# An expert-routed low-rank FFN: summing the extension's partial groups on GpSimd and choosing the expert on 32 partitions

## The chip, the cores and the metric

The kernel runs on one core of a Trainium2 chip. The metric is its device time in microseconds (us). The profile is of one execution of the program.

## The reference

x has 8 batches of 512 tokens with 2048 features. Each batch has an adapter (a LoRA pair chosen by an index). What is computed:

```
y   = x W^T + b + 2 (x A_slot) B_slot          # conditioning layer, rank 16
lg  = y route_w^T                              # 8 experts
e   = argmax(lg) ; w = lg[e]                   # top 1, first of equals
out = x + w * ((y A_e^T) Bw_e^T)               # rank 16 per expert
```

All of it is fp32 to a precision that needs products split in a high and a low part.

## The kernel before, in words

**Algebra.** y is never formed. P is the stack of the 8 experts' A (128 rows, "ER") and of route_w (8 rows), 136 columns in all ("PN"). A first stage computes M = W^T P^T (2048 x 136) from W in 32 pieces (lines 497 to 510), with `pt` as the moving operand. The 128 expert columns are split into `m_hi` and `m_lo` (fp32r), the 8 routing columns go to columns 0 to 7 of `ext` (two buffers), and the batch's LoRA A (16 columns) goes to columns 8 to 23 of it (GpSimd, line 292). A small matrix G per batch (`g_a`, `g_route`) carries the logits' unit rows, the LoRA B times P and the bias's products; its rows repeat with each 32-row group. It is made between pieces 23 and 24 of W (lines 527 to 537 on TensorE, 402 to 408 on VectorE), from `bp` and from `gz`.

**Units.** The second stage runs over 9 units: 7 batches of 512 tokens and the last batch in two halves of 256. x lies transposed: features on partitions, tokens along the free dimension. A batch has 8 pairs of 128-feature chunks. For a unit TensorE does, in this order (lines 561 to 622):

- the extension: 16 fp32 matmuls of 32 stationary columns, spread over four column groups so that `bank_e` holds four partial sums, one for each 32 rows (line 573);
- for each pair j = 0 to 7: six fp32r matmuls to `bank_h` (588 to 590: high by high, high by low, low by high), and from j = 1 on, behind them, the six matmuls of one output pair of the unit before (`out_pair`, 541 to 558), so that output pairs 0 to 5 lie beside main pairs 1 to 6;
- after j = 0: the logits, four small fp32 matmuls from `e_sb` (598). After j = 1: their transpose to tokens on partitions (604);
- after j = 7: the correction, three fp32r matmuls of G by e (608 to 610), then four transposes of `route` to `bank_r` (615), then output pairs 6 and 7 of the unit before.

**The order on the other engines** is written out by hand; each engine runs its instructions in that order and waits on semaphores.

ScalarE (354 to 377): `e_sb` from `bank_e` with the bias row's one added; x_hi of pairs 4 to 7; `logt_sb`; `e_hi` at j = 5; x_hi of the next unit's pairs 0 to 3; `h_sb` from `bank_h`; `wh_hi`. x_hi has a ring of four slots, and a slot is free when the main pair that read it is done (`t_main`).

VectorE (470 to 491): for j = 0 to 7 one x_lo (pairs 4 to 7 of this unit, then 0 to 3 of the next, line 425), from j = 1 to 6 one add (`add_x`, 465: output pair j - 1 plus x, which frees its bank), and at j = 1 `choose` (435 to 449: maximum over 8 logits, equality, preference for the first, one hot, times the maximum), at j = 3 `e_lo`. Then `weigh` (455), add 6, `wh_lo`, add 7. Pairs on `bank_out` use two banks in turn: an output pair may start when the pair two before it has been added (`pairs_added`, 197 to 203).

The sync engine's queue (228 to 255) loads W, then x in pieces of two pairs into a ring of 12, and stores the ring's pieces when both pairs are added.

## Time and profile before

| | |
|---|---|
| device time, median of 3 runs | 304.76 us (304.1 to 304.79) |
| span of the profiled execution | 302.6 us |
| TensorE matmul, busy | 295.9 us (98%) |
| VectorE, busy | 193.1 us (64%) |
| ScalarE, busy | 99.0 us (33%) |
| GpSimd, busy | 11.0 us (4%) |
| HBM | 54.60 MB read, 33.55 MB written, 291 GB/s |

The span runs from the first to the last instruction; the time outside it, some 2 us, is launch and end. The busy time of matmuls has their latency in it, and consecutive ones overlap in the record (each lasts 0.39 us and the next starts 0.23 us later), so a pace is read from starts. The trace gives each instruction with its start, its duration, its line and its tile, and in brackets the engine's idle time before it with what ended it. Line 382 and line 309 are helpers (VectorE's subtraction, ScalarE's copy): there the tile tells what it is.

### The profile page before, as it was taken

How to read it: one execution, taken by the hardware profiler on the slowest of the kernel's cores; microseconds unless marked ns; L12 is line 12 of the kernel's file. 1: busy time of each engine (PE TensorE's matmuls, PEld its weight loads, DVE VectorE, ACT ScalarE, POOL GpSimd, SP SyncE). 2: the span in 40 equal slices, each digit the busy share in tenths (PEclk: the TensorE clock that was granted, in tenths of full speed). 3: DMA queues.
4: the chain of work that ended last, by engine and by line, in shares of the span. 5: the costliest groups of instructions: out<-in, count | busy, mean ns of one | idle time of the engine just before them, and what ended most of it. 6: DMA issues, size and time to landing. Idle time of an engine off the chain costs nothing.

```text
span 302.6 us, 4629 instructions
## 1 busy us (share of the span) xinstructions
PE 295.9 (98%) x1857; PEld 233.5 (77%) x1857; DVE 193.1 (64%) x258; ACT 99.0 (33%) x147; POOL 11.0 (4%) x37
## 2 busy tenths in 40 slices
PE   7899999999999999999999999999999999999994
PEld 4899999997675885788488758866884787787994
DVE  0160000242894997498579839984985796698775
ACT  0020000223874332534253433424342533322410
POOL 6000300000100000000000000000000000000000
PEclk9999999999999999999999999999999999999999
DMA  7999999999920067739946991998399569536468
GB/s 245 400 404 394 415 412 411 414 417 418 421 107 2 25 252 259 298 133 388 418 172 237 417 405 54 379 395 337 118 377 417 202 220 406 208 151 266 178 218 299
DMA packets 20790, 88.44 MB, mean 292 GB/s; under 512 B 2210, under 2 KB 8354, under 8 KB 12962
## 3 DMA queue, kind: packets, MB, share of 16 engines
q1 hardware_dynamic: 18464, 86.06, 72.4%
q10 hardware_dynamic: 2306, 2.10, 2.0%
q8 instruction: 14, 0.23, 0.3%
q14 instruction: 6, 0.05, 0.0%
HBM read 54.60 MB, written 33.55 MB: 291 GB/s over the span
## 4 chain that ended last, share of the span: by engine, by line
PE 92%; DMA 3%; DVE 3%; SPq 1%; issue 0%
PE bank_out L508 18%; PE bank_h L588 11%; PE bank_h L590 10%; PE bank_h L589 10%; PE bank_e L573 9%; PE bank_out L555 9%; PE bank_out L557 9%; PE bank_out L556 9%; DMA w_ring<-W 3%; DVE x_ring L465 2%; PE bank_l L521 1%; PE bank_r L615 1%; PE bank_l L598 1%; PE bank_h L608 1%; PE bank_h L610 1%; PE bank_h L609 1%
## 5 line engine op out<-in xcount | busy, mean ns | idle before, releaser
L382 DVE TENSOR_TENSOR x_lo<-x_ring,x_hi 128x1024 fp32r<-128x1024 f32 (+1 forms) x72 | 78.9, 1106 | 41.1 <-ACT x_hi L309 41.1
L309 ACT ACTIVATE x_hi<-x_ring 128x1024 fp32r<-128x1024 f32 (+1 forms) x72 | 69.2, 966 | 85.8 <-PE bank_h L590 85.8
L465 DVE TENSOR_TENSOR x_ring<-bank_out,x_ring 128x1024 f32<-128x1024 f32 (+1 forms) x72 | 79.2, 1102 | 1.4 <-PE bank_out L557 1.1
L508 PE MATMUL bank_out<-pt,w_ring 128*128 128x136 f32 x512 | 60.6, 280 | 1.4 <-DMA w_ring<-W 1.4
L508 PEld LDWEIGHTS bank_out<-pt,w_ring 128*128 128x128 f32 x512 | 59.7, 190 | 2.8 <-DMA w_ring<-W 2.5
L588 PE MATMUL bank_h<-x_hi,m_hi 128*128 128x512 f32 (+1 forms) x144 | 55.1, 383 | 0.0
L555 PE MATMUL bank_out<-wh_hi,bw_hi 128*128 128x512 f32 (+1 forms) x144 | 54.6, 379 | 0.0
L590 PE MATMUL bank_h<-x_hi,m_lo 128*128 128x512 f32 (+1 forms) x144 | 53.3, 370 | 0.0
L556 PE MATMUL bank_out<-wh_lo,bw_hi 128*128 128x512 f32 (+1 forms) x144 | 53.2, 369 | 0.0
L557 PE MATMUL bank_out<-wh_hi,bw_lo 128*128 128x512 f32 (+1 forms) x144 | 53.2, 369 | 0.0
L589 PE MATMUL bank_h<-x_lo,m_hi 128*128 128x512 f32 (+1 forms) x144 | 53.1, 369 | 0.0
L588 PEld LDWEIGHTS bank_h<-x_hi,m_hi 128*128 128x128 f32 x144 | 27.0, 188 | 13.2 <-issue 8.5
L590 PEld LDWEIGHTS bank_h<-x_hi,m_lo 128*128 128x128 f32 x144 | 27.1, 188 | 5.0
L557 PEld LDWEIGHTS bank_out<-wh_hi,bw_lo 128*128 128x128 f32 x144 | 27.1, 188 | 5.0
L555 PEld LDWEIGHTS bank_out<-wh_hi,bw_hi 128*128 128x128 f32 x144 | 27.1, 188 | 4.8
L589 PEld LDWEIGHTS bank_h<-x_lo,m_hi 128*128 128x128 f32 x144 | 27.1, 188 | 4.6
L382 DVE TENSOR_TENSOR m_lo<-bank_out,m_hi 128x256 fp32r<-128x256 f32 x8 | 3.4, 424 | 42.5 <-ACT ext L309 42.5
L556 PEld LDWEIGHTS bank_out<-wh_lo,bw_hi 128*128 128x128 f32 x144 | 27.1, 188 | 4.2
L573 PE MATMUL bank_e<-x_ring,ext 128*32 128x512 f32 (+1 forms) x288 | 29.4, 548 | 0.0
L573 PEld LDWEIGHTS bank_e<-x_ring,ext 128*32 128x32 f32 x288 | 8.4, 109 | 16.4 <-issue 15.3
L309 ACT ACTIVATE m_hi<-bank_out 128x256 fp32r<-128x256 f32 x8 | 3.1, 383 | 44.4 <-PE bank_out L508 44.4
L356 ACT ACTIVATE e_sb<-bank_e,e_bias 128x512 f32<-128x512 f32 (+1 forms) x9 | 5.8, 642 | 25.9 <-PE bank_e L573 25.9
(77 smaller groups left out, 130.1 us busy)
## 6 DMA issues: line engine op xcount, KB each, us to landing
x_ring<-xT SPq DMA_DIRECT2D x32, 1024.0 KB, 9.0
outT<-x_ring SPq DMA_DIRECT2D x28, 1024.0 KB, 5.3
w_ring<-W SPq DMA_DIRECT2D x32, 512.0 KB, 9.0
outT<-x_ring SPq DMA_DIRECT2D x16, 256.0 KB, 2.4
pt<-PT SPq DMA_DIRECT2D x4, 272.0 KB, 5.8
x_ring<-loraB ACTq DMA_DIRECT2D x8, 128.0 KB, 10.6
la<-loraA ACTq DMA_DIRECT2D x8, 128.0 KB, 14.3
x_ring<-BwT SPq DMA_DIRECT2D x1, 1024.0 KB, 10.4
```

The source lines that it names most:

```text
L309: act.activation(out, in_, ACT.Copy).then_inc(done, 1)
L356: act.activation(e_sb[:, 0:nt], bank_e[:, 0:nt], ACT.Identity, bias=e_bias[:, 0:1]).then_inc(a_e, 1)
L382: dve.tensor_tensor(out, a, b, ALU.subtract).then_inc(done, 1)
L465: dve.tensor_tensor(x, out_banks(u, j), x, ALU.add).then_inc(v_out, 1)
L508: last = mm(bank_out[blk % 2][:, i, 0:PN], w_ring[:, n % WRING, o, i * P:(i + 1) * P], pt[:, k, :], start=(k == 0), stop=(k == C - 1))
L555: mm(out, bw_hi[:, o], hi, start=True, stop=False)
L556: mm(out, bw_hi[:, o], lo, start=False, stop=False)
L557: last = mm(out, bw_lo[:, o], hi, start=False, stop=True)
L573: last = mm(bank_e[g * GROUP:(g + 1) * GROUP, 0:nt], ext[u % 2][:, c, :], x_pair(u, c // 2)[:, c % 2, :], start=(r == 0), stop=(r == C // ...
L588: mm(h, m_hi[:, c, :], hi, start=(c == 0), stop=False)
L589: mm(h, m_hi[:, c, :], lo, start=False, stop=False)
L590: last = mm(h, m_lo[:, c, :], hi, start=False, stop=False)
```

## The change

- The order of P's columns is turned: the 8 routing columns come first, so that G is one tile `g_st` of 136 columns. Its rows 0 to 63 hold the high part and rows 64 to 95 the low part.
- ScalarE evicts the four partial groups of `bank_e` one by one to `e_part` (32 partitions, four groups beside each other), and GpSimd adds them (`add_groups`). ScalarE copies the sum's high part to rows 0 to 31 and 64 to 95 of `e_st`, VectorE writes the low part to rows 32 to 63 (`split_e`, at j = 1).
- After j = 4 TensorE does the logits in one fp32r matmul of g_st's first 128 columns by e_st (96 rows, 512 columns) and the correction in one more, to `bank_h`. The logit matmuls, their transpose and the three correction matmuls go.
- `choose` moves from j = 1 to j = 4 and works on 32 partitions: VectorE's 32x32 transpose of the logits, the same steps on 16 blocks of 8 instead of 4, high and low part of the maximum, the weights in `w_tok`, and a transpose back. ScalarE copies them to `w_er` ahead of the next unit's x_hi 3, and one fp32r matmul with a constant 0/1 matrix `spread` takes the place of the four route transposes.
- For `gz`, one matmul puts the bias's products in the right row of every group, and VectorE adds a constant; TensorE waits for it (`v_gz`) ahead of the G matmuls. z's matmul and ScalarE's copies z and gz go.

```diff
-        CHOOSE_AT, EHI_AT, ELO_AT = 1, 5, 3
+        EHI_AT, ELO_AT, LOG_AT, W_AT = 5, 1, 4, 3
+        SUMS = 3
+        TOPS = 9
 
...
+            def add_groups(u):
+
+                nt = UNITS[u][2]
+                part = e_part[:, :, 0:nt]
+                pool.wait_ge(a_e, NGROUPS * u + 2)
+                pool.tensor_tensor(part[:, 0, :], part[:, 0, :], part[:, 1, :], ALU.add).then_inc(g_sum, 1)
+                pool.wait_ge(a_e, NGROUPS * u + 4)
+                pool.tensor_tensor(part[:, 2, :], part[:, 2, :], part[:, 3, :], ALU.add).then_inc(g_sum, 1)
+                pool.wait_ge(g_sum, SUMS * u + 2)
+                pool.tensor_tensor(part[:, 0, :], part[:, 0, :], part[:, 2, :], ALU.add).then_inc(g_sum, 1)
+
+            pool.wait_ge(d_la0, 16 * 2)
+            load_ext(0)
+            load_ext(1)
+            for u in range(NU):
+                add_groups(u)
+                if u + 2 < NU:
+                    load_ext(u + 2)
...
+            copy(spread[:, :], spread0[:, :, :].rearrange("p e r -> p (e r)"), a_spread)
...
             for u, (b, _, nt) in enumerate(UNITS):
                 act.wait_ge(t_ext, u + 1)
-                act.activation(e_sb[:, 0:nt], bank_e[:, 0:nt], ACT.Identity, bias=e_bias[:, 0:1]).then_inc(a_e, 1)
+                act.activation(e_part[:, 0, 0:nt], bank_e[0:GROUP, 0:nt], ACT.Identity, bias=e_bias[:, 0:1]).then_inc(a_e, 1)
+                for g in range(1, NGROUPS):
+                    copy(e_part[:, g, 0:nt], bank_e[g * GROUP:(g + 1) * GROUP, 0:nt], a_e)
                 for j in range(SRING, NP2):
                     split_hi(u, j)
-                    if j == SRING:
-                        act.wait_ge(t_logt, u + 1)
-                        copy(logt_sb[0:nt // P * GROUP, :], bank_l[0:nt // P * GROUP, 0:P], a_log)
                     if j == EHI_AT:
-                        act.wait_ge(a_e, u + 1)
+                        act.wait_ge(g_sum, SUMS * (u + 1))
                         if u >= 1:
-                            act.wait_ge(t_h, u)
-                        copy(e_hi[:, 0:nt], e_sb[:, 0:nt], a_ehi)
-                if u + 1 < NU:
-                    for j in range(SRING):
+                            act.wait_ge(t_stack, u)
+                        copy(e_st[0:GROUP, 0:nt], e_part[:, 0, 0:nt], a_ehi)
+                        copy(e_st[2 * GROUP:3 * GROUP, 0:nt], e_part[:, 0, 0:nt], a_ehi)
+                for j in range(SRING):
+                    if j == W_AT:
+                        act.wait_ge(v_route, u + 1)
+                        if u >= 1:
+                            act.wait_ge(t_route, u)
+                        copy(w_er[0:GROUP, 0:nt], w_rows[:, 0:nt], a_w)
+                    if u + 1 < NU:
                         split_hi(u + 1, j)
-                act.wait_ge(t_h, u + 1)
+                act.wait_ge(t_main, NP2 * (u + 1))
                 if u >= 1:
                     act.wait_ge(v_whlo, u)
                 copy(h_sb[:, 0:nt], bank_h[:, 0:nt], a_h)
...
-                    dve.wait_ge(a_gz, 1)
+                    dve.wait_ge(t_pb, 1)
+                    dve.tensor_tensor(gz[:, :], bank_r[:, 0:PN], z_route[:, :], ALU.add).then_inc(v_gz, 1)
+                    dve.wait_ge(v_gz, 1)
...
+            def split_e(u):
+                nt = UNITS[u][2]
+                dve.wait_ge(a_ehi, 2 * u + 1)
+                if u >= 1:
+                    dve.wait_ge(t_stack, u)
+                sub(e_st[GROUP:2 * GROUP, 0:nt], e_part[:, 0, 0:nt], e_st[0:GROUP, 0:nt], v_elo)
+
             def choose(u):
 
-                q = UNITS[u][2] // P
-                over_e = lambda ap: ap.unsqueeze(2).broadcast_to([P, q, E])
-                over_r = lambda ap: ap.unsqueeze(3).broadcast_to([P, q, E, R])
-                seen = logits[:, 0:q, :]
+                nt = UNITS[u][2]
+                k = nt // GROUP
+                over_e = lambda ap: ap.unsqueeze(2).broadcast_to([GROUP, k, E])
+                seen = logt[:, 0:k, 0:E]
+                hi, lo = top_split[:, 0:k, 0], top_split[:, 0:k, 1]
                 dve.wait_ge(t_log, u + 1)
-                n = 5 * u
-                dve.tensor_reduce(top[:, 0:q], seen, AX_X, ALU.max).then_inc(v_top, 1)
+                n = TOPS * u
+                dve.transpose(logt[:, 0:k, :].rearrange("p k c -> p (k c)"), bank_l[0:GROUP, 0:nt]).then_inc(v_top, 1)
                 dve.wait_ge(v_top, n + 1)
-                dve.tensor_tensor(is_top[:, 0:q, :], seen, over_e(top[:, 0:q]), ALU.is_ge).then_inc(v_top, 1)
+                dve.tensor_reduce(top[:, 0:k], seen, AX_X, ALU.max).then_inc(v_top, 1)
                 dve.wait_ge(v_top, n + 2)
-                dve.tensor_tensor(score[:, 0:q, :], is_top[:, 0:q, :], prefer[:, :].unsqueeze(1).broadcast_to([P, q, E]),
+                dve.tensor_tensor(is_top[:, 0:k, :], seen, over_e(top[:, 0:k]), ALU.is_ge).then_inc(v_top, 1)
+                dve.tensor_copy(hi, top[:, 0:k]).then_inc(v_top, 1)
+                dve.wait_ge(v_top, n + 3)
+                dve.tensor_tensor(score[:, 0:k, :], is_top[:, 0:k, :], prefer[:, :].unsqueeze(1).broadcast_to([GROUP, k, E]),
                                   ALU.mult).then_inc(v_top, 1)
-                dve.wait_ge(v_top, n + 3)
-                dve.tensor_reduce(best[:, 0:q], score[:, 0:q, :], AX_X, ALU.max).then_inc(v_top, 1)
                 dve.wait_ge(v_top, n + 4)
-                dve.tensor_tensor(one_hot[:, 0:q, :], score[:, 0:q, :], over_e(best[:, 0:q]), ALU.is_equal).then_inc(v_top, 1)
+                dve.tensor_tensor(lo, top[:, 0:k], hi, ALU.subtract).then_inc(v_top, 1)
                 dve.wait_ge(v_top, n + 5)
-                if u >= 1:
-                    dve.wait_ge(t_route, u)
-                dve.tensor_tensor(route[:, 0:q, :, :], over_r(one_hot[:, 0:q, :]), over_r(over_e(top[:, 0:q])),
-                                  ALU.mult).then_inc(v_route, 1)
+                dve.tensor_reduce(best[:, 0:k], score[:, 0:k, :], AX_X, ALU.max).then_inc(v_top, 1)
+                dve.wait_ge(v_top, n + 7)
+                dve.tensor_tensor(one_hot[:, 0:k, :], score[:, 0:k, :], over_e(best[:, 0:k]), ALU.is_equal).then_inc(v_top, 1)
+                dve.wait_ge(v_top, n + 8)
+                dve.tensor_tensor(w_tok[:, 0:k, 0:2 * E].rearrange("p k (i e) -> p k i e", e=E),
+                                  one_hot[:, 0:k, :].unsqueeze(2).broadcast_to([GROUP, k, 2, E]),
+                                  top_split[:, 0:k, :].unsqueeze(3).broadcast_to([GROUP, k, 2, E]), ALU.mult).then_inc(v_top, 1)
+                dve.wait_ge(v_top, n + 9)
+                if u >= 1:
+                    dve.wait_ge(a_w, u)
+                dve.transpose(w_rows[:, 0:nt], w_tok[:, 0:k, :].rearrange("p k c -> p (k c)")).then_inc(v_route, 1)
...
+                    if j == LOG_AT:
                         choose(u)
-                    if j == ELO_AT:
-                        dve.wait_ge(a_ehi, u + 1)
-                        sub(e_lo[:, 0:UNITS[u][2]], e_sb[:, 0:UNITS[u][2]], e_hi[:, 0:UNITS[u][2]], v_elo)
                 weigh(u)
...
             pe.wait_ge(g_const, CONSTS)
-            mm(bank_r[0:1, 0:PN], ones[:, :], pb_sum[(C - 1) % 2][:, :], start=True, stop=True).then_inc(t_pb, 1)
+            mm(bank_r[:, 0:PN], to_bias_row[:, :, :].rearrange("p g j -> p (g j)"), pb_sum[(C - 1) % 2][:, :],
...
             pe.wait_ge(a_bp, 1)
-            pe.wait_ge(a_pb, 1)
-            mm(bank_l[:, 0:PN], place_z[:, :, :], z[:, :], start=True, stop=True).then_inc(t_gz, 1)
+            pe.wait_ge(v_gz, 1)
             for bank, b0, b1 in g_banks:
...
+                        last = mm(h, m_lo[:, c, :], hi, start=False, stop=(c == C - 1))
                     last.then_inc(t_main, 1)
...
-                    if j == 0:
-
-                        pe.wait_ge(a_e, u + 1)
+                    if j == LOG_AT:
+
+                        pe.wait_ge(a_ehi, 2 * (u + 1))
+                        pe.wait_ge(v_elo, u + 1)
                         if u >= 1:
-                            pe.wait_ge(v_top, 5 * u)
-                        for q in range(nt // P):
-                            last = mm(bank_l[q * GROUP:(q + 1) * GROUP, 0:P], g_route[:, b, :],
-                                      e_sb[:, q * P:(q + 1) * P], start=True, stop=True)
-                        last.then_inc(t_logt, 1)
-                    if j == 1:
-                        rows = nt // P * GROUP
-                        pe.wait_ge(a_log, u + 1)
-                        pe.transpose(bank_l[:, P:P + rows], logt_sb[0:rows, :], ident[0:rows, 0:rows]).then_inc(t_log, 1)
+                            pe.wait_ge(v_top, TOPS * (u - 1) + 1)
+                        mm(bank_l[:, 0:nt], g_st[0:STACK, b, 0:P], e_st[:, 0:nt], start=True, stop=True).then_inc(t_log, 1)
+                        mm(h, g_st[0:STACK, b, E:PN], e_st[:, 0:nt], start=False, stop=False).then_inc(t_stack, 1)
                     if u >= 1 and 1 <= j <= NP2 - HELD[u]:
                         out_pair(u - 1, j - 1)
-                pe.wait_ge(v_elo, u + 1)
-                mm(h, g_hi[:, b, :], e_hi[:, 0:nt], start=False, stop=False)
-                mm(h, g_hi[:, b, :], e_lo[:, 0:nt], start=False, stop=False)
-                mm(h, g_lo[:, b, :], e_hi[:, 0:nt], start=False, stop=True).then_inc(t_h, 1)
-                pe.wait_ge(v_route, u + 1)
+                pe.wait_ge(a_w, u + 1)
                 if u >= 1:
                     pe.wait_ge(v_wh, u)
-                for q in range(nt // P):
-                    last = pe.transpose(bank_r[:, q * P:(q + 1) * P], route[:, q, :, :].rearrange("p e r -> p (e r)"),
-                                        ident[:, :])
-                last.then_inc(t_route, 1)
+                else:
+                    pe.wait_ge(a_spread, 1)
+                mm(bank_r[:, 0:nt], spread[:, :], w_er[:, 0:nt], start=True, stop=True).then_inc(t_route, 1)
```

Left out: tile sizes and semaphores, GpSimd's constants, and the renamed column ranges of M.

## Rows read from the trace of the kernel before

**Rows 1.** The chain of work that ended last, by engine, share of span.
```profile
PE 92%; DMA 3%; DVE 3%; SPq 1%; issue 0%
```

**Rows 2.** Busy by stretch: length; PE, PEld, DVE, ACT, POOL; clock; DMA; GB/s.
```profile
76.80:89.90 13.10, 13.10 (x68) 10.14 (x64) 12.22 (x17) 10.44 (x13) 1.02 (x1) 1.00 0.64 267
149.30:177.20 27.90, 27.90 (x148) 19.99 (x144) 21.86 (x25) 10.98 (x13) 0.40 (x1) 1.00 0.77 302
```

**Rows 3.** TensorE in unit 2: start, us, engine, line, operation, out<-in, count.
```profile
117.81 3.64 PE L573 MATMUL bank_e<-x_ring,ext 128*32 128x512 f32 x32
121.39 0.50 PE L588 MATMUL bank_h<-x_hi,m_hi 128*128 128x512 f32 x1
...
122.65 0.40 PE L590 MATMUL bank_h<-x_hi,m_lo 128*128 128x512 f32 x1
...
123.67 0.39 PE L589 MATMUL bank_h<-x_lo,m_hi 128*128 128x512 f32 x1
...
125.16 0.39 PE L556 MATMUL bank_out<-wh_lo,bw_hi 128*128 128x512 f32 x1
...
126.32 0.40 PE L588 MATMUL bank_h<-x_hi,m_hi 128*128 128x512 f32 x1
...
142.19 0.39 PE L610 MATMUL bank_h<-e_hi,g_lo 128*128 128x512 f32 x1
...
143.09 0.39 PE L556 MATMUL bank_out<-wh_lo,bw_hi 128*128 128x512 f32 x1
```

**Rows 4.** ScalarE in unit 2: the same, idle before it in brackets.
```profile
121.52 0.69 ACT L356 ACTIVATE e_sb<-bank_e,e_bias 128x512 f32<-128x512 f32 x1 [3.85 <-PE bank_e L573]
123.08 1.06 ACT L309 ACTIVATE x_hi<-x_ring 128x1024 fp32r<-128x1024 f32 x1 [0.87 <-PE bank_h L590]
124.05 0.26 ACT L309 ACTIVATE logt_sb<-bank_l 128x128 f32<-128x128 f32 x1
...
127.92 1.06 ACT L309 ACTIVATE x_hi<-x_ring 128x1024 fp32r<-128x1024 f32 x1 [1.32 <-PE bank_h L590]
...
142.89 0.58 ACT L309 ACTIVATE h_sb<-bank_h 128x512 f32<-128x512 f32 x1
```

**Rows 5.** VectorE in unit 2: the same columns.
```profile
124.24 1.23 DVE L382 TENSOR_TENSOR x_lo<-x_ring,x_hi 128x1024 fp32r<-128x1024 f32 x1 [4.37 <-ACT x_hi L309]
...
128.46 0.18 DVE L435 TENSOR_REDUCE top<-bank_l 128x4 f32<-128x32 f32 x1
128.67 0.19 DVE L437 TENSOR_TENSOR is_top<-bank_l,top 128x32 f32<-128x32 f32 x1
...
129.58 0.69 DVE L448 TENSOR_TENSOR route<-one_hot,top 128x512 f32<-128x512 f32 x1
130.19 1.22 DVE L382 TENSOR_TENSOR x_lo<-x_ring,x_hi 128x1024 fp32r<-128x1024 f32 x1
131.32 1.22 DVE L465 TENSOR_TENSOR x_ring<-bank_out,x_ring 128x1024 f32<-128x1024 f32 x1
...
141.43 1.22 DVE L465 TENSOR_TENSOR x_ring<-bank_out,x_ring 128x1024 f32<-128x1024 f32 x1
```

**Rows 6.** GpSimd's copies; last, x_lo from 74 to 82 us: min/median/max ns.
```profile
33.29 1.89 POOL L284 COPY x_ring<-x_ring 128x2048 f32<-128x2048 f32 x1 [27.93 <-DMA x_ring<-loraB]
...
77.66 1.02 POOL L292 COPY ext<-la 128x256 f32<-128x256 f32 x1 [39.87 <-DMA la<-loraA]
...
121.55 0.40 POOL L292 COPY ext<-la 128x256 f32<-128x256 f32 x1 [27.33 <-PE bank_e L573]
...
L382 DVE TENSOR_TENSOR x_lo<-x_ring,x_hi x6: 1209/1222/1418, 74.9 to 81.6; 128x1024 fp32r<-128x1024 f32 x6
```

**Rows 7.** TensorE and VectorE around the end of piece 23 of W.
```profile
55.92 0.49 PE L533 MATMUL bank_l<-z,place_z 9*128 9x136 f32 x2
56.34 0.96 PE L536 MATMUL bank_e<-bp,x_ring 128*128 128x136 f32 x6
...
56.59 0.42 DVE L382 TENSOR_TENSOR m_lo<-bank_out,m_hi 128x256 fp32r<-128x256 f32 x1 [11.22 <-ACT ext L309]
```

## What the change will do: the prediction

> **What bounds the kernel now.** I read the chain of work first: TensorE carries 92% of it, and there is hardly a wait in it [rows 1]. Then the table by stretch: a full unit (512 tokens) lasts 27.9 us, TensorE is busy for all of it at full granted clock, VectorE for 21.86, ScalarE for 10.98, GpSimd for 0.40 [rows 2]. So matmul time that goes away can shorten a unit one for one, as long as the others keep up; and VectorE has only about 6 us to spare in each. Where those 6 us lie decides this case, so I then read one unit instruction by instruction, on TensorE [rows 3], ScalarE [rows 4] and VectorE [rows 5]. Most of VectorE's idle time is one gap at the start of the unit: it reaches its first x_lo of the unit at 124.24, 2.85 us after the first L588 at 121.39 [rows 3, 5]. From 128.46 on it is nearly full.
>
> **TensorE's part: about 1.05 us less per full unit.** From 126.32 to 142.19 there are 68 matmuls of 512 columns in fp32r, so one costs 0.233 us [rows 3]. The start-to-start times across the removed instructions, less the slots of what stays between, give what they cost: four logit matmuls 123.67 - 122.65 - 2 x 0.233 = 0.55; the logit transpose 125.16 - 123.67 - 6 x 0.233 = 0.09; four route transposes 143.09 - 142.19 - 2 x 0.233 = 0.43; three correction matmuls 0.70. Together 1.77. Added: two stacked matmuls and the spread, 3 x 0.233 = 0.70. (Their contraction is over 96 or 128 rows; no row has 96, and I see no reason for a different pace, as the 32-column L573 streams its operand at the normal rate.) Net 1.07. The walk below gives TensorE alone 26.85 where the measured unit has 27.9, so I use 1.05.
>
> **The unit walked through on all engines.** t = 0 is the first L588 of the unit; "n" is the next unit. TensorE: main pair 0 ends at 1.49, each later main or output pair takes 6 x 0.233 = 1.40, so main pair 4 ends at 1.49 + 7 x 1.40 = 11.29; stack to 11.76; out 3, main 5, out 4, main 6, out 5, main 7 to 20.16; spread to 20.39; out 6 to 21.79; out 7 to 23.19; extension (121.39 - 117.81 = 3.58, and 0.08 before it) to 26.85.
>
> VectorE's queue at j = 4 is now: x_lo(n,0), add 3, the whole of choose, x_lo(n,1), add 4, x_lo(n,2), add 5. ScalarE starts an x_hi 0.20 after the main pair that frees its slot (127.92 against 127.72, which is 126.32 + 1.40), and x_lo follows 1.16 after x_hi starts (124.24 against 123.08) [rows 3 to 5]. So x_lo(n,0) starts at 11.29 + 0.20 + 1.16 = 12.65. Neighbouring 1024-element operations start 1.135 apart (130.19 to 131.32) [rows 5]: add 3 at 13.79, choose at 14.92.
>
> How long is the new choose? Time follows elements per partition, not partitions: 32 elements take 0.19, 512 take 0.69, 1024 take 1.22, which is 0.155 + N/960; a dependent successor starts 0.035 after the end, an independent one 0.085 before it [rows 5]. The old one spans 130.19 - 128.46 = 1.73. The new one has 32 partitions and so four times the elements: 32x32 transpose of 512 elements 0.72, max over 128 0.32, is_top and copy 0.33, score and low part 0.33, best 0.32, one_hot 0.33, w_tok of 256 elements 0.46, transpose back 0.61 to its successor: 3.42. No row shows a DVE transpose. Below I bound it by 0.19 (the small operation), above by 1.22 (the row of twice the elements), and take the 512-element row, 0.69, since it reads and writes as many; hence choose between 2.4 and 4.5.
>
> Then x_lo(n,1) starts at 18.34, add 4 at 19.48, x_lo(n,2) at 20.61, add 5 at 21.75, and it ends at 22.97. Output pairs use two banks in turn (`pairs_added`), so out 7 must wait for add 5: it could start at 21.79 and starts at about 23.05. That is a stall of 1.26 us, larger than the 1.05 saved. Before, choose sat at j = 1, where output pairs were far from their banks' release, and add 5 at 141.43 ended 1.6 us before out 7's turn (144.26 by 143.09 + 5 x 0.233) [rows 3, 5]. What is queued behind choose thus waits with it: three x_lo, three adds, weigh and wh_lo. VectorE ends the unit at about 27.5, still ahead of its first x_lo in the next (26.85 + 1.26 + 3.4), so the delay does not grow from unit to unit. Without this wait, the next late thing would be a_w: v_route at 14.92 + 3.50, w_er copied after x_hi(n,2) by 19.3, 0.9 before TensorE asks for it.
>
> **GpSimd's sums and the port.** Four evictions on ScalarE replace one: 0.60 and 3 x 0.49 start to start, ends 0.13 + 2.16 = 2.3 [rows 4]. The sums are three adds of 512 elements with two inputs. No row shows one. GpSimd's copies cost 0.19 + 0.83 ns per element (0.40 for 256, 1.89 for 2048) [rows 6], so 0.62 is the floor; if two inputs take turns, 1.04; three turns with the result, 1.5, is the far end. I take 1.05, the middle case: sums at 1.35 to 2.40, 2.40 to 3.45, then 3.5. ScalarE waits for the last before the two e_st copies, x_hi 6 comes after, and the stack is needed only at 11.29. That has a cover of several us. The cost lies in the port: in unit 0 a copy on GpSimd took 1.02 instead of 0.40 while VectorE ran x_lo, and the x_lo beside it took 1.418 instead of 1.222 [rows 6]. So the two exclude each other for part of an instruction. Here sum 3 meets x_lo 4 and 5 (3.4 to 5.6): GpSimd waits to 4.6, x_lo 5 waits for GpSimd to 5.65, about 1.2 late. VectorE's queue up to add 2 (7 x 1.135 + 0.60 from 3.37) has 0.75 of slack before x_lo(n,0). So choose slips by 0.45, with the ext copy behind the sums by about 0.5; bounds 0 (no meeting) and 1.75 (sums of 1.5).
> The Trainium skill (SBUF — State Buffer, § Who interferes with whom) says that a VectorE instruction with two SBUF inputs contends with a GpSimd instruction that reads SBUF, and that the pair is an exclusive lock. The 1.02 against 0.40 agrees. It also speaks against this change in GPSIMD Engine Reference, § 3.1: about 2.6 cycles per element for a two-input add, from which I would estimate 1.25 us; with it the slip would be 0.9 and the whole about 3 us longer. No run so far shows it.
>
> A full unit then takes 26.85 + 1.26 + 0.5 = 28.6, 0.7 more than now. Six of them (units 1 to 6): +4.3 us.
>
> **Unit 0** has no output pairs: TensorE passes it in 13.1 us [rows 2], and choose's place, after main pair 4, leaves only three main pairs (4.2 us) until its result is asked for. By the same steps from 76.8 on, and with ScalarE busy with x_hi 0 to 3 until 77.5, its evictions end at 80.2, x_hi 4 and 5 at 82.1, sums and e_st by 84.3, stack to 84.95, x_hi(1,0) from 86.2, x_lo(1,0) from 87.6, choose from 88.75, v_route 92.25, w_er 92.85, spread to 93.15, extension from 93.2 where it was 89.9 (76.8 + 13.1): +3.3. With sums that wait for x_lo 3 and 4 and make x_lo 5 late it is up to +4.8. I take +4.0.
>
> **First stage.** z's matmul L533 goes (0.42), but TensorE now waits for v_gz before L536, and gz stands on VectorE behind m_lo of block 5, which runs at 56.59 for 0.42 [rows 7]. gz (136 elements, 0.30) ends at 57.2, L536 starts at 57.3 instead of 56.34 [rows 7]: +0.95. The stage is paced by TensorE, so it stays. The constants on GpSimd are about as many as before and done long before TensorE asks at 48 us; g_st is as long as g_hi. Zero, covered by the matmuls over W. If that cover were gone, it would be tenths of a us.
>
> **The half units** (7, 8): the same walk at half lengths gains 0.5 to 1 on TensorE and gives it back at the same wait, or at a_w in the last unit. Bounds -1 and +1 together; I take 0.
>
> **Sum.** 4.3 + 4.0 + 0.95 = +9.3 us on a span of 302.6, which stands about 2.2 below the median 304.76. That is a span of 311.9 and a time of 314.1; I say 313.5, as stalls that meet each other may be counted twice.
>
> **Rivals.**
> 1. VectorE's choose is short enough, and the gain comes through. With transposes at the floor of 0.19 and no port delay choose is 2.4: stall 0.25, six units -4.7, halves -0.7, unit 0 +2.3, first stage +0.95: about 302.5. The switch is at choose = 2.1, where the stall is nil, and about 2.7 for the total. For it: a new instruction without a row. Against: eight chained steps at the measured fixed 0.19 are 1.5 already, and elements are four times. Chance 0.13.
> 2. The walk holds, without port delays: stall 1.26, six units +1.4, unit 0 +3.3, +0.95: 310.4. Chance 0.22.
> 3. Transposes cost two cycles per element or sums are slow (over 1.3): choose up to 4.5, slip 1.2 to 1.75: six units at +2.3, unit 0 at +5.8: about 321. Chance 0.20.
> 4. The change does not do what it says, so that neither TensorE's saving nor the stall shows (304 to 306): 0.05.
> The forecast (311 to 317) has 0.40. The wait for choose in unit 0 leaves TensorE idle for 3 to 4 us; now it never is in this stage (granted clock 1.00 [rows 2]). Whether the clock falls after it no row shows; it would add a few us and lies in rival 3's range.
> **Range and chances.** 0.3% is about what a measurement can tell apart. Low end between rivals 1 and 2, high end at rival 3: 305 to 321. Faster 0.13 (rival 1), same 0.06 (rival 4 and the edge), slower 0.81.
>
> **What would show it.** TensorE's idle before L555 of out 7, ended by DVE L465, near 1.3 to 1.8 per full unit; units of 28.6; choose's chain of 3.4 between t_log and v_route; transposes of 0.7; sums near 1.05 and some x_lo longer than 1.22; an idle of 3 to 4 us ahead of the spread in unit 0; about 1 us ahead of L536. Wrong would be: transposes well below 0.5, or x_lo(n,0) starting much earlier than 1.4 after main pair 4.

## The result, and the profile after

| | before | after |
|---|---|---|
| device time, median | 304.77 us (304.1 to 304.92) | 319.0 us (316.97 to 320.78) |
| ratio, 95% interval | | 1.0474 (1.043 to 1.0518) |
| span of the profiled execution | 302.6 us | 319.0 us |
| TensorE, busy | 295.9 us (98%) | 294.2 us (92%) |
| VectorE, busy | 193.1 us (64%) | 215.8 us (68%) |
| GpSimd, busy | 11.0 us (4%) | 56.6 us (18%) |

The change makes the kernel 4.7% slower. The median is 5.5 us above the forecast of 313.5: inside the range of 305 to 321, and above the band of 311 to 317 to which the forecast gave its own chance. The profiled execution is the slowest of its four (320.78 us); what it has beyond the others is told with the clock below.

The page of after: the TensorE clock granted in 40 slices, and the chain of work that ended last, by engine, share of the span.

```profile
PEclk9999999999996999999999999999999999999998
...
DVE 38%; PE 35%; issue 13%; ACT 8%; DMA 2%; POOL 2%; SPq 0%; DVEq 0%; ACTq 0%; POOLq 0%
```

TensorE's 92% of the chain [rows 1] has become 35%, and VectorE leads. The one slice of low clock (95.7 to 103.7 us) lies at the end of unit 0 and over the extension behind it.

After by stretch, with the columns of [rows 2]: unit 0, the extension behind it in two parts, and the full units 1 and 2.

```profile
77.70:95.00 17.30, 12.47 (x54) 9.18 (x50) 14.95 (x20) 11.81 (x15) 6.56 (x4) 0.98 0.43 179
95.00:98.00 3.00, 2.76 (x13) 0.88 (x17) 3.00 (x4) 1.74 (x3) 0.00 (x0) 0.50 0.00 0
98.00:102.20 4.20, 4.20 (x25) 0.86 (x18) 1.20 (x2) 0.63 (x1) 0.00 (x0) 0.63 0.00 0
...
131.40:160.60 29.20, 27.53 (x132) 19.21 (x132) 24.65 (x29) 13.84 (x17) 6.04 (x4) 1.00 0.75 290
160.60:189.80 29.20, 27.54 (x132) 19.23 (x133) 24.63 (x29) 13.84 (x17) 6.02 (x4) 1.00 0.76 286
```

A full unit lasts 29.2 us where it was 27.9 [rows 2], and TensorE is now idle in it, for 1.7 us. VectorE's busy time there went from 21.86 to 24.65: by the share it still has 4.5 us to spare.

TensorE in unit 1 of after, which starts at 102.06. These are all the idle times that the profile counts in it: output pairs 6 and 7 wait for adds 4 and 5. (A wait read from starts is longer than the idle time in brackets, because the record of the matmul before it reaches into the wait.)

```profile
122.36 0.43 PE L652 MATMUL bank_r<-w_er,spread 128*128 128x512 f32 x1
123.87 0.50 PE L600 MATMUL bank_out<-wh_hi,bw_hi 128*128 128x512 f32 x1 [1.08 <-DVE x_ring L511]
...
126.14 0.50 PE L600 MATMUL bank_out<-wh_hi,bw_hi 128*128 128x512 f32 x1 [0.60 <-DVE x_ring L511]
```

VectorE in the same unit: two x_lo at the start, then the last add ahead of `choose`, choose's first and last steps, x_lo, add 4, add 5 and add 7.

```profile
105.78 3.66 DVE L410 TENSOR_TENSOR x_lo<-x_ring,x_hi 128x1024 fp32r<-128x1024 f32 x2 [5.89 <-ACT x_hi L335]
...
117.00 1.22 DVE L511 TENSOR_TENSOR x_ring<-bank_out,x_ring 128x1024 f32<-128x1024 f32 x1
118.13 0.70 DVE L473 STREAM_TRANSPOSE logt<-bank_l 32x512 f32<-32x512 f32 x1
118.86 0.28 DVE L475 TENSOR_REDUCE top<-logt 32x16 f32<-32x128 f32 x1
...
120.87 0.70 DVE L495 STREAM_TRANSPOSE w_rows<-w_tok 32x512 f32<-32x512 f32 x1
121.51 1.17 DVE L410 TENSOR_TENSOR x_lo<-x_ring,x_hi 128x1024 fp32r<-128x1024 f32 x1
122.61 1.20 DVE L511 TENSOR_TENSOR x_ring<-bank_out,x_ring 128x1024 f32<-128x1024 f32 x1
...
124.88 1.21 DVE L511 TENSOR_TENSOR x_ring<-bank_out,x_ring 128x1024 f32<-128x1024 f32 x1
...
129.47 1.21 DVE L511 TENSOR_TENSOR x_ring<-bank_out,x_ring 128x1024 f32<-128x1024 f32 x1
```

Only the first line has idle time in front. From 105.78 to 130.68 VectorE never waits; all its spare time lies ahead of its first x_lo. Add 4 ends at 123.81 and output pair 6 starts at 123.87; add 5 ends at 126.09 and output pair 7 starts at 126.14.

GpSimd in the same unit: the three sums, and the copy of `ext` behind them.

```profile
103.58 1.29 POOL L306 TENSOR_TENSOR e_part<-e_part 32x512 f32<-32x512 f32 x1 [17.07 <-ACT e_part L335]
104.83 1.29 POOL L308 TENSOR_TENSOR e_part<-e_part 32x512 f32<-32x512 f32 x1
106.20 2.16 POOL L310 TENSOR_TENSOR e_part<-e_part 32x512 f32<-32x512 f32 x1
108.31 1.38 POOL L299 COPY ext<-la 128x256 f32<-128x256 f32 x1
```

The third sum and the copy stand beside the two x_lo, and all of them are stretched: 2.16 instead of 1.29, 1.38 instead of 0.40 [rows 6], and 3.66 for the pair instead of two at 1.135 apart and 1.22 long [rows 5], 2.36.

**Where the 16.4 us of span are.** The table takes the start of the first main matmul of each unit (L588 before, L633 after). Units 1 to 5 are 29.2 each against 27.9.

| | before | after | more | predicted |
|---|---|---|---|---|
| first stage, up to unit 0 | 76.79 | 77.76 | +1.0 | +0.95 |
| unit 0, with the extension behind it | 16.7 | 24.3 | +7.6 | +4.0 |
| units 1 to 5 | 27.9 each | 29.2 each | +6.5 | +3.6 |
| unit 6 | 26.2 | 25.95 | -0.25 | +0.7 |
| units 7 and 8, to the end | 43.4 | 44.95 | +1.55 | 0 |

Unit 6 lost nothing, though it is a full unit: the x_lo behind its choose belong to unit 7, which has half the tokens, and they take 0.64 to 0.67 instead of 1.17 to 1.20. By starts, output pairs 6 and 7 then come 0.6 late together, and 2.2 in the units before.

### The profile page after: what moved, and what is told of

Same layout as the page of the kernel before. It is cut to its first block, busy times and chain, and to the rows that moved or that the text cites. A ratio compares the mean times of both kernels' runs of the same rounds, so it can differ in the third digit from the quotient of the medians.

```text
span 319.0 us, 4533 instructions
## 1 busy us (share of the span) xinstructions
PE 294.2 (92%) x1750; PEld 227.5 (71%) x1750; DVE 215.8 (68%) x292; ACT 121.7 (38%) x182; POOL 56.6 (18%) x67
## 4 chain that ended last, share of the span: by engine, by line
DVE 38%; PE 35%; issue 13%; ACT 8%; DMA 2%; POOL 2%; SPq 0%; DVEq 0%; ACTq 0%; POOLq 0%
PE bank_out L553 18%; DVE x_lo L410 16%; DVE x_ring L511 14%; PE bank_e L618 9%; ACT e_part L335 4%; ACT x_hi L335 3%; PE bank_out L600 2%; DMA w_ring<-W 2%; PE bank_out L602 2%; PE bank_out L601 2%; DVE logt L473 2%; PE bank_l L566 1%; DVE w_tok L489 1%; DVE one_hot L487 1%; DVE top L475 1%
## 5 line engine op out<-in xcount | busy, mean ns | idle before, releaser
L410 DVE TENSOR_TENSOR x_lo<-x_ring,x_hi 128x1024 fp32r<-128x1024 f32 (+1 forms) x72 | 87.9, 1237 | 35.0 <-ACT x_hi L335 34.6
L335 ACT ACTIVATE x_hi<-x_ring 128x1024 fp32r<-128x1024 f32 (+1 forms) x72 | 67.5, 960 | 44.8 <-PE bank_h L635 44.5
L600 PE MATMUL bank_out<-wh_hi,bw_hi 128*128 128x512 f32 (+1 forms) x144 | 55.4, 385 | 9.3 <-DVE x_ring L511 9.1
L633 PE MATMUL bank_h<-x_hi,m_hi 128*128 128x512 f32 (+1 forms) x144 | 54.2, 376 | 0.5 <-DVE x_lo L410 0.5
L306 POOL TENSOR_TENSOR e_part<-e_part 32x512 f32<-32x512 f32 (+1 forms) x9 | 11.0, 1218 | 212.1 <-ACT e_part L335 212.1
L633 PEld LDWEIGHTS bank_h<-x_hi,m_hi 128*128 128x128 f32 x144 | 27.1, 188 | 12.5 <-issue 6.7
L618 PE MATMUL bank_e<-x_ring,ext 128*32 128x512 f32 (+1 forms) x288 | 31.9, 586 | 0.0
L601 PEld LDWEIGHTS bank_out<-wh_lo,bw_hi 128*128 128x128 f32 x144 | 27.2, 189 | 3.9
## 6 DMA issues: line engine op xcount, KB each, us to landing
la<-loraA ACTq DMA_DIRECT2D x8, 128.0 KB, 14.2
```

The lines of the kernel that those rows point to most:

```text
L306: pool.tensor_tensor(part[:, 0, :], part[:, 0, :], part[:, 1, :], ALU.add).then_inc(g_sum, 1)
L335: act.activation(out, in_, ACT.Copy).then_inc(done, 1)
L410: dve.tensor_tensor(out, a, b, ALU.subtract).then_inc(done, 1)
L600: mm(out, bw_hi[:, o], hi, start=True, stop=False)
L601: mm(out, bw_hi[:, o], lo, start=False, stop=False)
L618: last = mm(bank_e[g * GROUP:(g + 1) * GROUP, 0:nt], ext[u % 2][:, c, :], x_pair(u, c // 2)[:, c % 2, :], start=(r == 0), stop=(r == C // ...
```

## The experiments

All times are medians, beside a median of 304.33 to 304.78 for before on the same chip. A unit's length is read from one first partial eviction of `bank_e` to the next.

### Is it the queue behind choose?

`x1_adds_first` keeps all work of the change and moves three of the next unit's x_lo on VectorE from between and behind adds 4 and 5 to behind add 5, the last add for which an output pair of the same unit waits.

```diff
-                    elif u + 1 < NU:
-                        split_lo(u + 1, j - SRING)
+                    elif j == SRING and u + 1 < NU:
+                        split_lo(u + 1, 0)
...
                         choose(u)
+                if u + 1 < NU:
+                    for j in range(1, SRING):
+                        split_lo(u + 1, j)
                 weigh(u)
```

> The changed kernel with one edit in VectorE's order: add 4 and add 5 stand directly behind choose, and x_lo 1 and 2 of the next unit behind them. No work is added or left out. Queue theory (output pair 7 waits for its bank until add 5, which stands behind choose and two x_lo): add 5 ends two x_lo, 2.27 us, earlier, TensorE's wait ahead of output pairs 6 and 7 (1.08 and 0.60 us now) goes, and units 1 to 5 fall from 29.2 to about 27.0 us; unit 0 stays. Time about 319 - 11 - 1 = 307 us. Port theory (what is lost is lost to GpSimd's sums, which make x_lo 4 and 5 late): the order behind choose doesn't matter, 317 to 321 us.

Measured: 305.84 us, 1.0064 (1.0038 to 1.0091) of before, units of 27.2. VectorE in unit 1 of it, around the last transpose of `choose`:

```profile
117.52 0.70 DVE L495 STREAM_TRANSPOSE w_rows<-w_tok 32x512 f32<-32x512 f32 x1
118.16 2.30 DVE L511 TENSOR_TENSOR x_ring<-bank_out,x_ring 128x1024 f32<-128x1024 f32 x2
120.40 3.46 DVE L410 TENSOR_TENSOR x_lo<-x_ring,x_hi 128x1024 fp32r<-128x1024 f32 x3
```

Adds 4 and 5 now follow choose at once, and the profile counts no idle time ahead of an output pair of a full unit (by starts, pairs 2 and 6 still come some 0.2 late each). The same instructions in another order give 13.2 us back of the 14.2 lost: 2.0 in each of five full units, 1.6 in units 6 and 7. The rest, some 1.6, is within what the clock does to the kernel after from one execution to the next (below) and is not shown to come from the order. That the order of VectorE's queue was what cost the full units their time is shown.

`x2_no_sums` takes GpSimd's sums away; e_st is made from the first partial group alone, so the sum over the other three is left out.

```diff
-                add_groups(u)
...
-                        act.wait_ge(g_sum, SUMS * (u + 1))
+                        act.wait_ge(a_e, NGROUPS * (u + 1))
```

> The changed kernel without GpSimd's three sums per unit: e_st is made from the first partial group alone (the sum over the other three groups is left out), all else stays. Port theory as a part of the cost: x_lo 4 and 5 take 1.22 us each again (3.66 us for the two now, 2.36 without), choose starts 1.1 to 1.3 us earlier, full units fall to about 28.0 us, and unit 0 loses its waits ahead of main pair 4 and the stack (0.47 and 1.45). Time 319 - 6 - 2 = 311 us, or about 308 if the wait ahead of the spread then is short enough to leave the clock up. Queue theory alone (no part for the port): 317 to 321 us. If the sums were all of the loss: below 305 us.

Measured: 308.61 us, 1.0141 (1.0105 to 1.0176), units of 28.07. So 1.13 of a unit's length hangs on the sums and their collision with x_lo. Choose in the unit that starts at 153.75:

```profile
168.66 0.69 DVE L472 STREAM_TRANSPOSE logt<-bank_l 32x512 f32<-32x512 f32 x1
```

It starts 14.91 into the unit, where the walk of the prediction has 14.92 ahead of any slip, and 1.16 earlier than in after (118.13 - 102.06 = 16.07). One idle time of 0.6 ahead of output pair 7 is left; read from starts, pairs 6 and 7 come 1.28 late in all. Choose in its place costs that without any sum beside it.

### Is it choose's place, or its length?

Four kernels. `x5_short_choose` shortens choose in after (the preference for the first of equal logits is left out, three steps of it). `x6_before_choose4` moves the old choose of before to the new place. `x10_before_long4` and `x11_before_long1` pad the choose of before with two more multiplications of 512 elements, at the new and at the old place.

```diff
-                dve.tensor_tensor(score[:, 0:k, :], is_top[:, 0:k, :], prefer[:, :].unsqueeze(1).broadcast_to([GROUP, k, E]),
-                                  ALU.mult).then_inc(v_top, 1)
...
-                dve.tensor_reduce(best[:, 0:k], score[:, 0:k, :], AX_X, ALU.max).then_inc(v_top, 1)
...
-                dve.tensor_tensor(one_hot[:, 0:k, :], score[:, 0:k, :], over_e(best[:, 0:k]), ALU.is_equal).then_inc(v_top, 1)
```

> The changed kernel with three of choose's dependent steps left out (score, best, one_hot: the preference for the first of equal logits isn't computed, the equality with the maximum is used in its place). Choose then spans about 2.7 us instead of 3.38. Queue theory: each tenth of a us off choose is a tenth off each full unit, so units 1 to 5 fall by 0.65 to 0.75 to about 28.5 us, unit 0 by as much: 4 to 5 us in all, 314 to 315 us. If choose were hidden: no change in the unit's length.

Measured: 314.57 us, 1.0309 (1.028 to 1.0338), units of 28.62. Choose is 0.6 shorter (116.08 to 118.87, 2.79 instead of 3.38) and so is the unit. Its length goes into a full unit one for one, as the walk had it.

The edit of `x6_before_choose4`, on before:

```diff
-        CHOOSE_AT, EHI_AT, ELO_AT = 1, 5, 3
+        CHOOSE_AT, EHI_AT, ELO_AT = 4, 5, 3
```

> The kernel before with choose moved in VectorE's queue from j = 1 to j = 4, behind add 3, where the changed kernel has it; its work and everything else stay. Place alone, with the old length of 1.73 us: by the walk add 5 ends near 22.0 us into the unit and output pair 7's turn is at 22.9, so there is no stall, a full unit stays at 27.9 us and the time at 304.3 us. If the place by itself were the cause, pair 7 would wait and the unit be longer by 1 us or more (over 310 us).

Measured: 304.94 us, 1.0011 (0.9997 to 1.0026), units of 27.9. The move by itself costs nothing.

The padding, in both other kernels; `x10_before_long4` has the move of x6 as well:

```diff
+                for i in range(2):
+                    dve.tensor_tensor(route[:, 0:q, :, :], over_r(one_hot[:, 0:q, :]), over_r(over_e(top[:, 0:q])),
+                                      ALU.mult).then_inc(v_top, 1)
+                    dve.wait_ge(v_top, n + 6 + i)
```

> The kernel before with choose at j = 4 and two more 512-element multiplications in it that write the same result again, so that it spans about 3.2 us instead of 1.73; nothing else of the change is in it. Queue theory: place and length together make the loss. Choose from about 15.6 to 18.8 us into the unit, add 5 ends at 23.4, 0.6 us after output pair 7's turn at 22.9: full units at 28.5 to 28.6 us, 4 us more, 308 to 309 us. If the loss in the changed kernel came from anything else in it (evictions, sums, stacked operand), this kernel would stay at 304.5.

Measured: 310.5 us, 1.0196 (1.0174 to 1.0218), units of 28.65. That is 1.5 to 2.5 above what was expected: the full units are as forecast to 0.1, but unit 0 is 1.6 longer than before (17.69 against 16.13) and unit 7 0.7, and the forecast had neither. The padded choose lasts 3.18 (138.84 to 142.02, where the next operation starts), and in that unit output pair 7 waits for add 5, with 0.47 of idle time.

> The same long choose in the kernel before, at its old place j = 1. VectorE then has about 1.2 us of idle time and slack behind it before output pair 7 asks for add 5, and add 5 ends about 0.6 us ahead of its turn: full units stay at 27.9 us, 304.5 us. If length alone decided, it would be as slow as at j = 4.

Measured: 311.52 us, 1.0228 (1.0206 to 1.025), units of 28.73: a clear miss. TensorE's wait in unit 2 of `x11_before_long1`, and VectorE ahead of it:

```profile
136.31 0.50 PE L559 MATMUL bank_out<-wh_hi,bw_hi 128*128 128x512 f32 x1 [0.56 <-DVE x_ring L469]
```

```profile
133.29 0.69 DVE L452 TENSOR_TENSOR route<-one_hot,top 128x512 f32<-128x512 f32 x1
133.90 1.22 DVE L382 TENSOR_TENSOR x_lo<-x_ring,x_hi 128x1024 fp32r<-128x1024 f32 x1
135.04 1.22 DVE L469 TENSOR_TENSOR x_ring<-bank_out,x_ring 128x1024 f32<-128x1024 f32 x1
```

Behind the long choose (it ends at 133.98) come one x_lo and add 1, which ends at 136.26, and output pair 3 waits for that. The prediction says that at j = 1 "output pairs were far from their banks' release". That is wrong: a unit is 0.83 longer (28.73 against 27.9), and the padding is 1.45 (3.18 against 1.73), so there was only some 0.6 of slack. With x6 and x10 it follows that in the kernel before the length of choose does the harm at either place, and the place alone does none.

### The waits around unit 0, and the clock

`x3_gz_early` makes `gz` one block of W earlier on VectorE.

```diff
-                if n == G_AT // NWH:
+                if n == BP_AT // NWH:
                     dve.wait_ge(t_pb, 1)
                     dve.tensor_tensor(gz[:, :], bank_r[:, 0:PN], z_route[:, :], ALU.add).then_inc(v_gz, 1)
+                if n == G_AT // NWH:
                     dve.wait_ge(v_gz, 1)
```

> The changed kernel with the gz addition one block earlier in VectorE's queue, ahead of m_lo of block 5 instead of behind it. Its operands are there since 48.4 us, so TensorE's wait of 1.38 us ahead of L581 goes: 1.0 to 1.4 us less, 317.8 us, against a scatter of the changed kernel of about 2 us either way; the idle time in the trace decides. Rival (the wait comes from something else, the W pieces or bp): the idle time stays.

TensorE between pieces of W, first in after, then in `x3_gz_early`:

```profile
49.79 6.19 PE L553 MATMUL bank_out<-pt,w_ring 128*128 128x136 f32 x52
57.36 0.93 PE L581 MATMUL bank_e<-bp,x_ring 128*128 128x136 f32 x6 [1.38 <-DVE gz L431]
```

```profile
49.80 5.61 PE L554 MATMUL bank_out<-pt,w_ring 128*128 128x136 f32 x47
55.24 0.86 PE L582 MATMUL bank_e<-bp,x_ring 128*128 128x136 f32 x6
```

The wait of 1.38 is gone. Measured: 316.62 us (315.81 to 318.55), 1.0421 (1.0379 to 1.0464), 2.4 below after; the scatter of both is wider than the wait, so only the lines show its size.

`x4_keep_busy` puts 12 matmuls without use into TensorE's idle time ahead of unit 0's spread.

```diff
+                if u == 0:
+                    pe.wait_ge(v_bw, 1)
+                    for _ in range(12):
+                        mm(bank_out[0][:, 0, :], bw_hi[:, 0:P], bw_hi[:, 0:T], start=True, stop=True)
                 pe.wait_ge(a_w, u + 1)
```

> The changed kernel with twelve extra matmuls of constants into an output bank that nobody reads before it is overwritten, in unit 0 between main pair 7 and the spread, where TensorE now idles for 3.16 us. They take 12 x 0.233 = 2.8 us and end before w_er is there. Clock theory (the idle time in unit 0 lets the granted clock fall to 1.2 GHz, and the extension behind it takes 6.16 us instead of 3.64): the extension takes 3.6 us again, the granted clock is 1.00 in that stretch, time about 316 us with less scatter. Rival (the extension of unit 1 is slow for another reason, as an operand that comes late): it stays at 6.2 us, and the time at 319 us.

TensorE at the end of unit 0, in after, then in `x4_keep_busy`:

```profile
95.24 0.79 PE L652 MATMUL bank_r<-w_er,spread 128*128 128x512 f32 x1 [3.16 <-ACT w_er L335]
95.97 6.16 PE L618 MATMUL bank_e<-x_ring,ext 128*32 128x512 f32 x32
```

```profile
91.24 2.91 PE L650 MATMUL bank_out<-bw_hi 128*128 128x512 f32 x12
94.54 0.50 PE L656 MATMUL bank_r<-w_er,spread 128*128 128x512 f32 x1 [0.39 <-ACT w_er L335]
94.98 3.64 PE L618 MATMUL bank_e<-x_ring,ext 128*32 128x512 f32 x32
```

Measured: 317.29 us (317.17 to 317.66), 1.0424 (1.0403 to 1.0446). That is 1.3 above the 316 expected, and no faster than the one execution of after with a mean granted clock of 0.999 (316.97). In after, TensorE was idle for 3.16, the clock granted from 95 to 98 was 0.50 (the level of 1.2 GHz), and the extension took 6.16. With the filler it took 3.64 at the level of 2.4 GHz, as before [rows 3]. The scatter falls from 3.8 us to 0.5. The fall comes in some executions only: in the profiles of x1 and x3 the same idle time (3.14 and 3.13) is followed by an extension of 3.64, while in those of x2 and x5 idle times of 2.63 and 2.81 are followed by one of 5.34. It costs up to 2.8 us (6.16 - 3.64, and 0.3 on the spread), most of the 3.8 between the four times of after; these also stand in the order of their mean granted clocks: 316.97 at 0.999, 318.77 at 0.994, 319.22 at 0.990, 320.78 at 0.985.

### A version that beats both

`x7_all` has x1 and x3, moves the last x_lo too, and puts unit 0's spread behind unit 1's extension.

```diff
+            def spread_out(u):
...
                 last.then_inc(t_ext, 1)
+                if u == 1:
+                    spread_out(0)
...
                 if u >= 1:
+                    spread_out(u)
```

> The changed kernel with three edits of order, no work added or left out: gz one block earlier on VectorE; choose, add 4 and add 5 ahead of all four x_lo of the next unit; and in unit 0 the spread behind unit 1's extension instead of ahead of it, so that TensorE has 3.6 us of work while choose runs. Queue theory: full units at 27.0 to 27.2 us, the two waits of 1.4 and 3.1 us gone and with the second the fall of the clock: 305.8 - 1.2 - 3.1 = 301 to 302 us, some 1% below the kernel before. Rival (a wait takes the place of the one removed: x_lo 0 of the next unit or a_w is late): 304 us or more.

Measured: 303.23 us, 0.9953 (0.9939 to 0.9967), units of 27.0. It is 0.5% faster than before, but 1.2 us above the upper end of what was expected. TensorE's idle times from 94 to 107 us in it, both ahead of unit 0's output pairs:

```profile
97.43 0.47 PE L602 MATMUL bank_out<-wh_hi,bw_hi 128*128 128x512 f32 x1 [1.14 <-DVE wh_lo L410]
104.86 0.50 PE L602 MATMUL bank_out<-wh_hi,bw_hi 128*128 128x512 f32 x1 [1.62 <-DVE x_ring L512]
```

`x8_all_tail` also puts one of the last unit's held output pairs ahead of its spread:

```diff
+                for j in range(NP2 - HELD[u], NP2 - 1) if u == NU - 1 else ():
+                    out_pair(u - 1, j)
```

> As the run before it, and in the last unit output pairs 5 and 6 stand ahead of the spread instead of behind it: TensorE waits there about 2 us for w_er. The pairs fill 1.4 us of it: 1 to 1.4 us less, about 300 us. Rival: weigh and wh_lo of the last unit then come later and take the gain back, no change.

Measured: 302.64 us, 0.9937 (0.9921 to 0.9953). A gain of 0.6 where 1 to 1.4 was expected. The last unit shows where the rest went, in `x7_all`, then in `x8_all_tail`:

```profile
287.52 0.38 PE L614 MATMUL bank_r<-w_er,spread 128*128 128x256 f32 x1 [1.54 <-ACT w_er L335]
```

```profile
290.01 0.36 PE L602 MATMUL bank_out<-wh_hi,bw_hi 128*128 128x256 f32 x1 [0.90 <-DVE wh_lo L410]
```

The wait for w_er is filled, and one for wh_lo, behind it, takes its place: the rival of the expectation, in part. It has the lowest median of the kernels here that compute all of it, 0.6% below before; `x9_mid` below is not told apart from it.

`x9_mid` puts unit 0's spread inside unit 1's extension, so that weigh and wh_lo start sooner:

```diff
+                    if u == 1 and r == 1:
+                        spread_out(0)
                 last.then_inc(t_ext, 1)
-                if u == 1:
-                    spread_out(0)
```

> The fast variant with the tail edit, and unit 0's spread in the middle of unit 1's extension instead of behind it. In the variant without this, w_er is there at 91.4 us, while the extension runs from 89.4 to 93.0, and weigh, the four evictions of unit 1 and so its output pairs 0 and 2 come late (waits of 1.14 and 1.62 us on TensorE). With the spread 1.7 us earlier these two waits shrink: 1 to 2.5 us less than 302.6, about 301 us. Rival (the waits come from the sums alone): no change.

Measured: 302.92 us, 0.9947 (0.9927 to 0.9966), no gain over x8. The idle time ahead of the first output pair fell from 1.14 to 0.60, but the pair starts no sooner: 0.96 behind unit 1's first eviction in both. The spread now waits inside the extension, and weigh starts 1.24 ahead of that eviction in both: on VectorE it stands behind the four x_lo of unit 1 (91.3 to 95.9), not behind the spread. So the edit only moved the wait. The other one stayed at 1.61.

`x12_fast_no_sums` is x8 without the sums, by the edit of x2, so that e_st is again made from the first partial group alone.

> The fast variant with the tail edit, without GpSimd's three sums per unit (e_st from the first partial group alone, the sum over the other three left out). In the changed kernel the sums cost about 1.1 us per full unit by making x_lo 4 and 5 late. If that cost reached the end only through VectorE's full queue ahead of output pair 7, it is nil now that full units run at TensorE's pace: units 2 to 5 stay at 27.0 us, and only unit 0 and 1 lose their waits (0.45, 1.46, 1.62): 302.6 - 2 to 3.5 = 299 to 300.5 us. If the collisions still cost something in every unit, the full units fall below 26.9 and the time to 296 or less.

Measured: 297.26 us, 0.9757 (0.9724 to 0.9789), units of 26.8. VectorE's first two x_lo of unit 1, in `x12_fast_no_sums` and then in `x8_all_tail`:

```profile
97.82 2.36 DVE L409 TENSOR_TENSOR x_lo<-x_ring,x_hi 128x1024 fp32r<-128x1024 f32 x2 [2.74 <-ACT x_hi L334]
100.10 1.22 DVE L511 TENSOR_TENSOR x_ring<-bank_out,x_ring 128x1024 f32<-128x1024 f32 x1
```

```profile
100.55 3.66 DVE L410 TENSOR_TENSOR x_lo<-x_ring,x_hi 128x1024 fp32r<-128x1024 f32 x2 [2.74 <-ACT x_hi L335]
104.13 1.21 DVE L512 TENSOR_TENSOR x_ring<-bank_out,x_ring 128x1024 f32<-128x1024 f32 x1
```

Without the sums the pair takes 2.36, 1.30 less, and TensorE's wait for the add behind it shrinks from 1.63 to 0.33. So even where the full units are free of waits the sums cost 5.4 us, some 2.4 in unit 0 and 1.3 in unit 1. This was 2 to 3 us more than expected. The last 0.2 of each full unit (27.0 against 26.8) is a wait too short to show as idle time. In unit 3 of `x8_all_tail`, TensorE at output pair 2:

```profile
159.09 0.40 PE L648 MATMUL bank_h<-x_hi,m_lo 128*128 128x512 f32 x1
159.41 0.50 PE L602 MATMUL bank_out<-wh_hi,bw_hi 128*128 128x512 f32 x1
159.75 0.39 PE L603 MATMUL bank_out<-wh_lo,bw_hi 128*128 128x512 f32 x1
```

The two steps take 0.32 and 0.34 where 0.23 is the pace, 0.20 too much; add 0, behind the stretched pair of x_lo, ends at 159.35. In `x12_fast_no_sums` the same steps take 0.24 and 0.23.

## Why the prediction was right, and where it was off

**The direction and its cause were right.** TensorE's saving is real, and adds held up behind choose take more than it. The forecast's sign test, TensorE idle ahead of output pair 7, is there; the predicted figure of 1.3 to 1.8 is met by 1.68, though in two waits (1.08 ahead of pair 6, 0.60 ahead of pair 7), as add 4 was late already. The walk had pair 6 start at once.

**TensorE's saving** was right to 0.1: the walk gives TensorE alone 26.85 in a full unit, and x12, where the profile counts no idle time in them, has units of 26.8. The 27.0 of x7 and the 27.2 of x1 are the same work and the short waits read from starts above.

**The stall without the sums** was right as well: 1.26 in the walk, 1.28 by starts in x2, and 26.85 + 1.26 = 28.1 is the 28.07 of x2.

**choose** was predicted at 3.42 with transposes of 0.69; it measured 3.38 with 0.70. The 512-element row was the right one.

**The slack in front of choose was mis-sized.** This is the term that failed. I had the collision with the sums right: x_lo 5 "about 1.2 late", measured 1.30. I then took 0.75 of it as covered and put the slip at 0.45. In x2, add 2 starts at 165.12, so the next operation could start 1.135 later, at 166.25, and x_lo 0 of the next unit starts at 166.39: the slack is 0.14. So 1.30 - 0.14 = 1.16 comes through, and choose starts 16.07 into the unit in after against 14.91 in x2. The slack went in two places. The four evictions take 2.43 from the first to x_hi 4 (102.21 to 104.64), where I had 2.07, so that VectorE's first x_lo starts at 3.72 and not 3.37; and from add 0 to the x_lo behind the low part of e_st it takes 1.96 (109.36 to 111.32), where I had 1.135 + 0.60. With it the unit adds up, by starts: output pairs 2, 6 and 7 come 0.2, 1.35 and 0.85 late, and 26.8 + 2.4 = 29.2, where I had 26.85 + 1.76 = 28.6.

**The sums** were taken at 1.05 each, the middle between bounds of 0.62 and 1.5. They take 1.29 alone and 2.16 beside x_lo. The error is real, but it is worth only the step from 1.2 to 1.30 in the collision.
The Trainium skill (GPSIMD Engine Reference, § 3.1) puts a two-input add at about 2.6 cycles per element, from which the prediction quoted an estimate of 1.25 us; the trace agrees with 1.29. Its lock between the two engines (SBUF — State Buffer, § Who interferes with whom) is borne out as well, by 3.66 against 2.36.

**Unit 0** was predicted at +4.0 and took +7.6. The idle times ahead of the stack and of the spread were in the walk in kind (0.6 and 3 to 4), the one ahead of main pair 4 (0.47) was not; the one at the stack is 1.45. Without the fall of the clock the unit would be at +4.8, the figure that the prediction gave as its upper one, for sums that make x_lo late; in x4, with the filler, it is (20.88 against 16.13). The rest, 2.8, is the clock, which I had put into rival 3's range and not into the sum.

**First stage:** +0.95 predicted, +1.0 measured, and x3 shows the cause. **Units 6 to 8:** predicted +0.7 and 0, measured -0.25 and +1.55. Unit 6 was walked as if the x_lo behind its choose were of full length; the last unit has +1.45, with a wait of 1.55 for w_er in it, the a_w of the prediction, which I had bounded at 1 for both halves together. The two misses partly cancel, and that is luck.

**The rivals.** Rival 1 (the gain comes through) needs a choose under 2.7 and is out. Rival 2 (no port delay) is what x2 shows, 28.07 a unit. Rival 3 (slower parts) came near in its slip (1.16 against 1.2 to 1.75) and in its clock, but not by its conditions: transposes of 0.70, sums of 1.29. Its figure of 321 is also wrongly added: 6 x 2.3 + 5.8 + 0.95 = 20.6 on 304.76 is 325, so the upper end of the range stands on a wrong sum. The result is inside all the same. The profiled span is 7.1 above the 311.9 of the sum: 2.9 in units 1 to 5 (the slack), 2.8 the clock, 0.8 the rest of unit 0, 0.6 in units 6 to 8. And 313.5 instead of the 314.1 of the sum was a deduction for stalls counted twice, which nothing here bears out.

**A wrong reason beside a right sum:** that the old place was far from any bank release. x11 refutes it. In the kernel before, a choose nearly as long as the new one costs as much at the old place as at the new one (28.73 against 28.65 a unit), and my sentence on the old place would have sent a reader to mend the wrong thing.

## What to carry to other kernels

When work moves to an engine that is not the bound, walk that engine's queue up to each instruction on which the bound engine waits: here VectorE was busy for 68% of the span and yet had no slack from its first x_lo to its last add. Put work whose result is needed late (the next unit's x_lo) behind work that releases a bank; the same instructions in that order were 13.2 us faster, 11.6 of them in the lengths of units 1 to 7. When a delay is said to be covered, work out the slack of the whole queue in front of it: 0.14 was there and not 0.75, and that was most of what each full unit took beyond the forecast. Count what a move to 32 partitions adds: choose grew by 1.65 (1.73 to 3.38), of which its two transposes are 1.37; the small steps on four times the elements, 0.28 each instead of 0.19, make a smaller part.

## What the runs showed of the hardware

- GpSimd's two-input add of 512 fp32 elements takes 1.29 us, against 0.40 for a copy of 256 and 1.89 for one of 2048 [rows 6]. Beside VectorE's x_lo it takes 2.16, and the two x_lo take 1.30 longer: the delay is nearly the length of one sum.
- VectorE's 32x32 transpose of 32x512 fp32 takes 0.70 us, from PSUM and from SBUF alike. Its other operations of 512 elements per partition take about as long, on 32 partitions (the low part of e_st, 0.68) as on 128 (the old `route`, 0.69 [rows 5]).
- After the same idle time of about 3.1 us TensorE's granted clock fell to its 1.2 GHz level in one profile and not in two others; after 2.63 and 2.81 us the extension behind took 5.34 instead of 3.64 in two more. A kernel with such a gap scatters (3.8 us here), and filling the gap takes the scatter away (0.5 us).
